# Graph layers of a relational graph network with expert layers: weight products of a finished tile spread over other couples, and a mask on numbers that are waited for

## The chip, the core and the metric

The kernel runs on one core of a Trainium2 chip. TensorE (PE) multiplies, VectorE (DVE) and ScalarE (ACT) work element by element, GpSimd (POOL) issues the gathers, and SyncE (SP) issues transfers and, in the graph layers, passes on counts. The metric is the time of one execution in microseconds. Each engine has a sequencer, which reads the program, executes register instructions and branches itself, and hands the rest to the engine.

## The reference

```python
def _rgcn_conv(x, W, Wroot, b, src, dst, etype):        # N = 6250, R = 8, 256 wide, 100000 edges
    xs = x[src]
    seg = dst * R + etype
    sums = jax.ops.segment_sum(xs, seg, num_segments=N * R)
    cnt = jax.ops.segment_sum(jnp.ones_like(xs[:, 0]), seg, num_segments=N * R)
    mean = (sums / jnp.maximum(cnt, 1.0)[:, None]).reshape(N, R, -1)
    return x @ Wroot + b + jnp.einsum('nrd,rde->ne', mean, W)

# _L0_gnn_ref
h = _rgcn_conv(x, W1, Wroot1, b1, src, dst, edge_type)
h = jax.nn.relu(h)
h = _rgcn_conv(h, W2, Wroot2, b2, src, dst, edge_type)

# the whole
x = x + _L0_gnn_ref(_layernorm(x), edge_index, edge_type_8, ...)
x = x + _L0_ffn_ref(_layernorm(x)[None], ...)[0]        # 8 experts, each row to its best 2
```

The targets `dst` are drawn with a squared uniform, so that nodes with low numbers have many edges and those with high numbers few.

## The kernel before, in words

**Stages.** The first 0.14 ms sort the edges by target and relation and normalize the rows. Then come the two graph layers, and from about 2300 us the expert layers, which the change leaves as they are (only the type of a small table of counts is another).

**A graph layer.** The sorted edges lie in 784 blocks of 128. POOL gathers each block's source rows by one indirect transfer (line 450) into a ring of 16 slots. SP waits for each landing and for each slot's last reader, and passes both on as counts (lines 355 and 362). The 6250 nodes are 49 tiles of 128. A tile is 8 windows of 16 nodes times 8 relations, so that a window has 128 sums. Two windows are a couple, and a tile has 4 couples, k = 0 to 3. For each window PE multiplies two blocks with a selection matrix of zeros and ones that DVE makes (`sel`, line 890; two matmuls a block, lines 1234 and 1235). A window that spans more than two blocks runs a loop over the further ones (`more_sums`, line 1237), with matrices that DVE makes in a loop of its own (`sel_more`, line 898). Which block comes first in a window and how many follow is read from a table into registers at each tile's start (line 1227), on PE and on DVE.

**After a couple's sums.** PE's first weight product behind them raises `sums_done`. DVE then takes the counts' inverse (layer 1), the selections of the couple after next (line 890) and those of further blocks of the next couple; ACT scales the sums to means in half precision and DVE their remainder (lines 589 and 933). One couple later PE turns the means by 8 transposes (line 1246, `turn`), and ACT copies them to `means` (line 561, counted by `means_in`).

**The weight products.** When the four couples of a tile are turned, they are multiplied by the weights: 18 parts (8 relations and the root, two halves each) of 3 matmuls (line 1254). They are strewn between the blocks of the next tile and of the one after: `couple` gives each couple a list of parts, and `spread` says how many stand at each of five places: behind the first block of the first window, behind its second, behind its further blocks, behind the first block of the second window, and behind all sums. The list is 2 parts at k = 1, 6 at k = 2 and 5 at k = 3 of the next tile, and 5 at k = 0 of the one after. Between the sums and the parts of k = 1, PE waits for `means_in`. Tiles 0 and 1 are written out, the others are a loop over pairs of tiles (`graph_tiles`). `turn`, `product` and `sums_out` (DVE's read of a finished tile's products) are the other names that matter below.

**Register instructions.** A wait for a count that depends on the table needs the number computed first: in `couple` the first block plus 2, in `more_sums` the count before plus 1, in `more_blocks` (DVE) the block plus 1, and on SP a number loaded from `free_meta`.

Of the kernel before, what the change touches and what calls it, by code (L numbers as in the profile page):

```python
def build_program(nc, x, src, dst, edge_type, gnn_w, gnn_root, gnn_bias,
# [5 lines left out]
    f32, f16, i32 = mybir.dt.float32, mybir.dt.float16, mybir.dt.int32  # L7
# [31 lines left out]
    PITCH = 2 * D + 4  # L39
    WSH, KSH = WIN.bit_length() - 1, P.bit_length() - 1  # L40
# [21 lines left out]
    PART_PAIRS = ((0, 0), (0, 1), (1, 0))  # L62
    Z_BITS, TOP, X_BITS = 8, 13, 8
# [13 lines left out]
    with ctx:  # L77
# [60 lines left out]
        lot_meta = sb("lot_meta", [1, X + 1, 4], i32)  # L138
# [176 lines left out]
        def _(sp):  # L315
# [34 lines left out]
            for layer in range(2):  # L350
# [7 lines left out]
                with sp.Fori(0, TURNS - 1) as u:  # L358
                    sp.load(regs, free_meta[0:1, ds(u * RING, RING)])
                    for s in range(RING):  # L360
                        sp.wait_ge(steps_done[layer], sp.snap(regs[s], donate=True, min_val=1, max_val=BLOCKS + 3 * WINDOWS))
                        sp.sem_inc(slots_free[layer], 1)
                        landed(u if s < AHEAD else u + 1, (s + AHEAD) % RING)
# [149 lines left out]
        def _(act):  # L513
# [45 lines left out]
            for layer in range(2):  # L559
# [19 lines left out]
                def tile_work(t, par, age):  # L579
                    for k in range(STEPS):  # L580
# [7 lines left out]
                        for h in range(2):  # L588
                            act.activation(mean16[:, slot, h, 0:D], ps_sum[slot][h][:, 0:D], ACT.Copy, scale=inv[:, ds(c * 2 + h, 1)]).then_inc(mean_high[layer], 1)  # L589
                        if age > 0 or k > 0:  # L590
                            act.wait_ge(turn_done[layer], c)
                            turned(1 - slot, par if k else 1 - par, (k - 1) % STEPS)
                        if layer == 0:
# [3 lines left out]
                            if k == 2 and age == 2:  # L597
                                relu_rows(t - 2, par)
# [91 lines left out]
        def _(v):  # L690
# [187 lines left out]
            def load_meta(w, count):  # L878
# [3 lines left out]
                lo = [v.snap(regs[2 * k], donate=True, min_val=0, max_val=BLOCKS - 1) for k in range(count)]  # L882
# [6 lines left out]
            def first_blocks(layer, lo, w, slot, h):  # L889
                return v.scalar_tensor_tensor(sel[:, slot, h], lane16[:].unsqueeze(1).to_broadcast([P, 2, P]), win_off[:, ds(w, 1)],  # L890
                                              key_tab[:, ds(lo, 2)].unsqueeze(2).to_broadcast([P, 2, P]), ALU.add, ALU.is_equal)

            def more_blocks(layer, lo, since, upto, w):
                with v.If(upto > since):
                    with v.Fori(0, upto - since) as i:
                        block = (lo + i + 2).with_bounds(min_val=0, max_val=BLOCKS - 1)
                        v.wait_ge(rows_ready[layer], block + 1)
# [3 lines left out]
            for layer in range(2):  # L901
# [11 lines left out]
                def tile_work(t, par, age):  # L913
                    regs, lo, mark = load_meta(t * WPT + 2, WPT + 2)
                    for k in range(STEPS):
# [19 lines left out]
                        if k == 1 and age == 2:  # L935
                            sums_out(t - 2, par)
                        if layer == 0:
# [4 lines left out]
                            if k == 2:  # L942
# [233 lines left out]
        def _(pe):  # L1176
# [47 lines left out]
            def load_meta(w):  # L1224
# [3 lines left out]
                lo = [pe.snap(regs[2 * k], donate=True, min_val=0, max_val=BLOCKS - 1) for k in range(WPT)]  # L1228
                return regs, lo, [pe.snap(regs[2 * k + 1], donate=True, min_val=0, max_val=BLOCKS) for k in range(WPT + 1)]

            for layer in range(2):
# [19 lines left out]
                def product(par, part):  # L1251
# [3 lines left out]
                                      start=part == 0 and n == 0, stop=part == PARTS - 1 and n == 2, skip_group_check=True)  # L1255
# [163 lines left out]
```

## Time and profile before

| | |
|---|---|
| median of 3 runs | 3062.41 us (3062.01 to 3065.25) |
| profiled execution, first to last instruction | 3064.4 us |
| PE matmul / PE weight load busy | 77% / 58% |
| DVE / ACT / POOL busy | 58% / 38% / 60% |
| layer 1 of the graph, gathers to last product | about 141 to 1199 us |
| layer 2 of the graph | about 1207 to 2290 us |

### The profile page before, as it was taken

The page shows a single profiled execution, that of the slowest core. Times are in us where ns is not written, and L with a number is a line of the kernel's source. Part 1 is how long each engine was busy: PE and PEld are TensorE (multiplying, and loading weights), DVE is VectorE, ACT ScalarE, POOL GpSimd, SP SyncE. Part 2 cuts the span into 40 slices and gives each one's busy share as a digit, 9 for nine tenths or more (in the row PEclk, how much of TensorE's full clock was granted, in tenths as well). Part 3 has the DMA queues.
Part 4 walks back from the last instruction along what each step waited for, and adds up shares of the span by engine and source line. Part 5 has one row for each costly group of instructions (what it writes and reads, how often), then busy time and mean ns, then how long its engine had stood idle before and what let it go on. Part 6 is the DMA issues. An engine that isn't in the chain of part 4 may idle for free.

```text
span 3064.4 us, 82720 instructions
## 1 busy us (share of the span) xinstructions
PE 2352.2 (77%) x19212; PEld 1776.0 (58%) x19213; DVE 1782.2 (58%) x4944; ACT 1167.6 (38%) x2306; POOL 1836.5 (60%) x1908
## 2 busy tenths in 40 slices
PE   1456777778888887456777888888987189999999
PEld 0123444555666775123445556667776178888888
DVE  7434445555566664333445555656666278877777
ACT  5001223334445553011223344455542165655554
POOL 1777777766666553777777777666536623333333
PEclk9556789999999998557899999999995599999999
DMA  7343333333333321333343444333335432322222
GB/s 244 100 130 105 108 108 108 109 101 99 97 94 93 90 88 58 106 99 115 115 119 118 123 122 125 112 113 111 106 110 192 146 123 86 100 72 72 72 72 61
DMA packets 164416, 331.14 MB, mean 108 GB/s; under 512 B 35518, under 2 KB 101786, under 8 KB 164216
## 3 DMA queue, kind: packets, MB, share of 16 engines
q0 software_dynamic: 90864, 245.38, 26.9%
q1 hardware_dynamic: 39608, 41.02, 4.5%
q10 hardware_dynamic: 33872, 43.92, 4.5%
q8 instruction: 27, 0.44, 0.1%
q14 instruction: 45, 0.37, 0.0%
HBM read 283.29 MB, written 49.07 MB: 108 GB/s over the span
## 4 chain that ended last, share of the span: by engine, by line
PE 48%; POOL 24%; issue 15%; DVE 7%; DMA 3%; DVEq 2%; ACT 1%; POOLq 0%; SPq 0%; ACTq 0%
POOL ring L450 20%; PE more_banks L1254 15%; PE sum_banks L1392 8%; PE sum_banks L1234 7%; PE sum_banks L1235 5%; PE sum_banks L1382 4%; PE more_banks L1382 4%; POOL lot_in L470 3%; PE more_banks L1246 3%; DMA ring<-table,row_tab 2%; DVE sel L890 1%; DMA out<-edge_work,lot_ids 1%; PE more_banks L1366 1%; DVEq L881 1%; DVE weights L1072 0%
## 5 line engine op out<-in xcount | busy, mean ns | idle before, releaser
L450 POOL DMA_INDIRECT ring<-table,row_tab x1568 | 1509.2, 963 | 703.8 <-issue 339.0
L1254 PE MATMUL more_banks<-weights,stage 128*128 128x256 f16 x5292 | 846.9, 283 | 7.8 <-ACT stage L561 4.5
L589 ACT ACTIVATE stage<-sum_banks,inv 128x256 f16<-128x256 f32 x784 | 327.4, 471 | 815.5 <-DVE inv L923 398.7
L1254 PEld LDWEIGHTS more_banks<-weights,stage 128*128 128x128 f16 x5292 | 502.4, 101 | 144.9 <-issue 71.6
L1234 PE MATMUL sum_banks<-ring,sel 128*128 x1568 | 449.3, 287 | 161.1 <-DVE sel L890 84.2
L898 DVE TENSOR_SCALAR sel_more<-lane,win_off,key_tab 128x128 f16 x780 | 268.8, 345 | 443.4 <-SPq L355 371.2
L1234 PE MATMUL sum_banks<-ring,sel_more 128*128 x780 | 244.3, 314 | 350.0 <-DVE sel_more L898 193.8
L890 DVE SCALAR_TENSOR_TENSOR sel<-lane,win_off,key_tab 128x256 f16<-128x256 f16 x792 | 349.4, 482 | 240.4 <-PE more_banks L1254 235.8
L1235 PE MATMUL sum_banks<-ring,sel 128*128 x1568 | 448.7, 287 | 0.0
L561 ACT ACTIVATE stage<-more_banks 128x1024 f16<-128x1024 f16 x392 | 402.7, 1027 | 15.1 <-PE more_banks L1246 14.9
L1234 PEld LDWEIGHTS sum_banks<-ring,sel_more 128*128 x780 | 78.4, 100 | 529.7 <-issue 524.9
L933 DVE SCALAR_TENSOR_TENSOR stage<-sum_banks,inv,stage 128x256 f16<-128x256 f32 x784 | 345.4, 479 | 25.8 <-issue 13.3
L1234 PEld LDWEIGHTS sum_banks<-ring,sel 128*128 128x128 f16 x1568 | 157.4, 100 | 266.5 <-issue 240.5
L489 POOL DMA_INDIRECT out<-edge_work,lot_ids x106 | 108.1, 1019 | 325.0 <-DVE edge_work L1160 308.7
L587 ACT ACTIVATE stage<-sum_banks 128x256 f16<-128x256 f32 x196 | 75.1, 383 | 591.3 <-DVE inv L923 302.1
L1235 PE MATMUL sum_banks<-ring,sel_more 128*128 x780 | 261.2, 336 | 0.0
L1246 PE MATMUL more_banks<-ident,stage 128*128 128x128 f16 x3136 | 257.3, 229 | 0.1
L665 ACT ACTIVATE stage<-sum_banks,edge_work,undo 128x256 f32<-128x256 f32 x212 | 113.0, 561 | 315.6 <-PE sum_banks L1382 294.1
L1246 PEld LDWEIGHTS more_banks<-ident,stage 128*128 128x128 f16 x3136 | 223.3, 103 | 14.0 <-DVE stage L933 1.2
L1392 PE MATMUL sum_banks<-weights,edge_work 128*128 128x256 f16 x1824 | 208.1, 275 | 7.5 <-DVE edge_work L1144 7.5
L920 DVE TENSOR_SCALAR inv<-sum_banks 128x2 f32 (+1 forms) x196 | 31.2, 159 | 290.6 <-PE more_banks L1254 276.1
L1392 PEld LDWEIGHTS sum_banks<-weights,edge_work 128*128 128x128 f16 x1824 | 179.5, 99 | 29.9 <-issue 8.4
(287 smaller groups left out, 2763.0 us busy)
## 6 DMA issues: line engine op xcount, KB each, us to landing
ring<-table,row_tab POOLq DMA_INDIRECT x1568
weights<-L_ffn_W ACTq DMA_DIRECT2D x96, 178.5 KB
stage<-L_ffn_W ACTq DMA_DIRECT2D x16, 1024.0 KB, 5.5
edge_work<-lot_in SPq DMA_DIRECT2D x54, 260.0 KB, 2.7
table<-edge_work SPq DMA_DIRECT2D x7, 896.0 KB, 4.4
table<-edge_work ACTq DMA_DIRECT2D x49, 128.0 KB
out<-acc SPq DMA_DIRECT2D x6, 1024.0 KB
acc<-x SPq DMA_DIRECT2D x6, 896.0 KB, 11.0
```

Of the source, the lines that this page charges most:

```text
L450: pool.indirect_dma_start(ring_rows[:, b % RING, 0:2 * D], None, tables[layer], bass.IndirectOffsetOnAxis(row_tab[:, b:b + 1], 0)).then_in ...
L561: act.activation(means[:, par, :, :, 2 * k * WIN:(2 * k + 2) * WIN].rearrange("p q r (v n) -> p v (q r) n", v=2), ps_turn[slot].rearrange( ...
L589: act.activation(mean16[:, slot, h, 0:D], ps_sum[slot][h][:, 0:D], ACT.Copy, scale=inv[:, ds(c * 2 + h, 1)]).then_inc(mean_high[layer], 1)
L890: return v.scalar_tensor_tensor(sel[:, slot, h], lane16[:].unsqueeze(1).to_broadcast([P, 2, P]), win_off[:, ds(w, 1)], key_tab[:, ds(lo, 2 ...
L898: v.tensor_scalar(flat(sel_more[:, ds(block & (RING - 1), 1), :]), lane16[:], win_off[:, ds(w, 1)], key_tab[:, ds(block, 1)], ALU.add, ALU ...
L933: v.scalar_tensor_tensor(mean16[:, slot, h, D:2 * D], ps_sum[slot][h][:, 0:D], inv[:, ds(c * 2 + h, 1)], mean16[:, slot, h, 0:D], ALU.mult ...
L1234: pe.matmul(to[:, 0:D + 1], hot, flat(slot[:, :, D:2 * D + 1]), start=first, stop=last, skip_group_check=True)
L1235: return pe.matmul(to[:, 0:D], hot, flat(slot[:, :, 0:D]), start=False, stop=last, skip_group_check=True)
L1246: out = [pe.transpose(ps_turn[slot][:, (4 * h + q) * P:(4 * h + q + 1) * P], mean16[:, slot, h, q * P:(q + 1) * P], ident16[:]) for h in r ...
L1254: return [pe.matmul(ps_out[par], rows[:, xp * KD + k, :], w16[:, wp, k, r * D:(r + 1) * D], start=part == 0 and n == 0, stop=part == PARTS ...
L1382: ins = pe.matmul(hid_bank[c % 4], up_sb[slot][:, wp, k, c * P:(c + 1) * P], lotT[:, zp, k, :], start=k == 0 and (wp, zp) == PART_PAIRS[0] ...
L1392: ins = pe.matmul(bank[2 + h][:, 0:D], hidT[:, hp, c, h * P:(h + 1) * P], down_sb[slot][:, wp, c, :], start=c == 0 and (hp, wp) == PART_PA ...
```

## The change

It has four parts. (1) The parts of a tile are given out as 4 at k = 2 and 5 at k = 3 of the next tile, and 5 at k = 0 and 4 at k = 1 of the one after, with the root's two parts first (`PART_ORDER`). (2) The wait for `means_in` stands at the start of k = 2, ahead of its sums. (3) DVE's `sums_out` moves from k = 1 to k = 2 and its addition of the second bias from k = 2 to k = 1; ACT's `relu_rows` moves from behind the turned copy at k = 2 to ahead of it at k = 3. (4) Every number that an engine waits for is put through `& MASK` (2047), and the bounds on the table's block numbers move to where they are used as addresses. `lot_meta` becomes a table of 16-bit integers. The end of a layer has 9 parts of the last tile but one instead of 5, and 2 parts of the last tile, ahead of the last wait.

```diff
+    MASK = (1 << (BLOCKS + 3 * WINDOWS).bit_length()) - 1
...
+    PART_ORDER = [R * KD + k for k in range(KD)] + list(range(R * KD))
+    SHARES = (5, 4, 4, 5)
+    SPREAD = {4: (1, 1, 0, 1, 1), 5: (1, 1, 1, 1, 1)}
+    CUTS = (0, SHARES[2], SHARES[2] + SHARES[3], SHARES[2] + SHARES[3] + SHARES[0], PARTS)
...
# SP
-                        sp.wait_ge(steps_done[layer], sp.snap(regs[s], donate=True, min_val=1, max_val=BLOCKS + 3 * WINDOWS))
+                        sp.wait_ge(steps_done[layer], sp.snap(regs[s], donate=True) & MASK)
...
# ACT, tile_work
+                        if layer == 0 and k == 3 and age == 2:
+                            relu_rows(t - 2, par)
                         if age > 0 or k > 0:
                             act.wait_ge(turn_done[layer], c)
                             turned(1 - slot, par if k else 1 - par, (k - 1) % STEPS)
...
-                            if k == 2 and age == 2:
-                                relu_rows(t - 2, par)
...
# DVE, more_blocks
                     with v.If(upto > since):
+                        held = v.snap(lo & MASK)
                         with v.Fori(0, upto - since) as i:
...
-                        v.wait_ge(rows_ready[layer], block + 1)
+                        v.wait_ge(rows_ready[layer], held + i + 3)
...
# DVE, tile_work
-                        if k == 1 and age == 2:
+                        if k == 2 and age == 2:
                             sums_out(t - 2, par)
...
-                            if k == 2:
+                            if k == 1:
                                 here = flat(acc[:, ds(t, 1), :])
                                 v.tensor_tensor(here, here, bias_bc[:, 1, :], ALU.add).then_inc(x_biased, 1)
...
# PE, more_sums
                     with pe.If(upto > since):
+                        done = pe.snap(since & MASK)
                         with pe.Fori(0, upto - since) as i:
-                            pe.wait_ge(more_ready[layer], since + i + 1)
+                            pe.wait_ge(more_ready[layer], done + i + 1)
...
# PE, couple
-                    if k == 0:
-                        parts = [(par, n) for n in range(PARTS - 5, PARTS)] if age == 2 else []
-                    else:
-                        parts = [(1 - par, n) for n in (range(0, 2), range(2, 8), range(8, 13))[k - 1]] if age > 0 else []
-                    spread = ((1, 1, 1, 1, 1), (0, 0, 0, 0, 2), (1, 1, 1, 1, 2), (1, 1, 1, 1, 1))[k]
+                    due = (k + 2) % STEPS
+                    of, enough = (par, age == 2) if k < 2 else (1 - par, age > 0)
+                    parts = [(of, n) for n in PART_ORDER[CUTS[due]:CUTS[due + 1]]] if enough else []
+                    spread = SPREAD[SHARES[k]]
...
+                    if k == 2 and age > 0:
+                        if age == 1:
+                            pe.wait_ge(w_split, layer + 1)
+                        pe.wait_ge(means_in[layer], t * STEPS)
...
-                        pe.wait_ge(rows_ready[layer], lo[j] + 2)
+                        pe.wait_ge(rows_ready[layer], (lo[j] & MASK) + 2)
...
-                    if k == 1 and age > 0:
-                        if age == 1:
-                            pe.wait_ge(w_split, layer + 1)
-                        pe.wait_ge(means_in[layer], t * STEPS)
...
# PE, the end of a layer
-                for n in range(PARTS - 5, PARTS):
+                for n in PART_ORDER[CUTS[2]:CUTS[3]]:
+                    product(1, n)
+                turn(COUPLES - 1, 1)
+                for n in PART_ORDER[CUTS[3]:]:
                     ins = product(1, n)[-1]
                 ins.then_inc(out_done[layer], 1)
-                turn(COUPLES - 1, 1)
+                for n in PART_ORDER[:KD]:
+                    product(0, n)
                 pe.wait_ge(means_in[layer], COUPLES)
                 if layer == 0:
                     weights_spread(1)
-                for n in range(PARTS):
+                for n in PART_ORDER[KD:]:
                     ins = product(0, n)[-1]
```

```order
L1278 REGISTER_ALU
L1280 REGISTER_ALU [waits rows_ready0]
L1234 REGISTER_ALU [waits sel_ready0]
L1234 ISA
L1234 MATMUL sum_banks<-ring,sel 128x257
L1235 ISA
L1235 MATMUL sum_banks<-ring,sel 128x256
L1234 REGISTER_ALU x2
L1234 ISA
L1234 MATMUL sum_banks<-ring,sel 128x257
L1235 ISA
L1235 MATMUL sum_banks<-ring,sel 128x256
```

The same place now.

```order
L1289 REGISTER_ALU x2
L1291 REGISTER_ALU [waits rows_ready0]
L1241 REGISTER_ALU [waits sel_ready0]
L1241 ISA
L1241 MATMUL sum_banks<-ring,sel 128x257
L1242 ISA
L1242 MATMUL sum_banks<-ring,sel 128x256
L1262 MATMUL more_banks<-weights,stage 128x256 x3
L1241 REGISTER_ALU x2
L1241 ISA
L1241 MATMUL sum_banks<-ring,sel 128x257
L1242 ISA
```

There is one register instruction more ahead of the wait for `rows_ready`, and a weight part of 3 matmuls stands behind the first block, where nothing stood. A second such instruction stands ahead of the second window's wait; over a tile's body PE has the same 138 matmuls and 16 more REGISTER_ALU, one in each of its 8 windows and one in each of the 8 further-block branches.

**PE, the end of couple k = 1 in layer 1's loop, before** (`means_in0` counts layer 1's turned copies, `mean_low0` its remainders).

```order
L1239 ISA
L1239 COMPARE_AND_BRANCH
L1238 UNCONDITIONAL_BRANCH
L1254 MATMUL more_banks<-weights,stage 128x256 [waits means_in0]
L1254 MATMUL more_banks<-weights,stage 128x256 x5
L1245 ISA
L1246 MATMUL more_banks<-ident,stage 128x128 [waits mean_low0]
L1246 MATMUL more_banks<-ident,stage 128x128 x7
```

What stands between the turn of k = 1 and the first block of k = 2 now, where the wait has gone.

```order
L1254 MATMUL more_banks<-ident,stage 128x128 x7
L1281 ISA
L1281 MATMUL sum_banks<-ident,edge_work 128x128
L1281 ISA
L1281 MATMUL sum_banks<-ident,edge_work 128x128
L1289 REGISTER_ALU [waits means_in0]
L1289 REGISTER_ALU
L1291 REGISTER_ALU [waits rows_ready0]
L1241 REGISTER_ALU [waits sel_ready0]
L1241 ISA
```

The wait stands on a register instruction ahead of k = 2, behind the turn and the root's transposes, no longer on the products behind the sums of k = 1; those are 3 matmuls now and were 6.

**DVE, a branch for further blocks in layer 2, before and now.**

```order
L894 COMPARE_AND_BRANCH
L895 UNCONDITIONAL_BRANCH
L895 ISA
L898 REGISTER_ALU [waits rows_ready1]
L898 REGISTER_ALU
L898 ISA
L898 TENSOR_SCALAR sel_more<-lane,win_off,key_tab 128x128
L895 ISA
```

```order
L900 COMPARE_AND_BRANCH
L902 UNCONDITIONAL_BRANCH
L904 REGISTER_ALU
L904 ISA
L905 ISA [waits rows_ready1]
L905 REGISTER_ALU
L905 ISA
L905 TENSOR_SCALAR sel_more<-lane,win_off,key_tab 128x128
L902 ISA
```

One register instruction more stands in the branch ahead of the loop, and in the loop the number that is waited for comes from an ISA instead of a REGISTER_ALU.

## Rows read from the trace of the kernel before

**Rows 1.** The page, part 4: shares of the span on the chain that ended last.

```profile
PE 48%; POOL 24%; issue 15%; DVE 7%; DMA 3%; DVEq 2%; ACT 1%; POOLq 0%; SPq 0%; ACTq 0%
```

**Rows 2.** By stretch, gathers (L450) alone: from:to us, POOL busy (count), PEclk, DMA share, GB/s.

```profile
300.00:586.00 286.00, 216.86 (x228) 0.87 0.37 108
586.00:1190.00 604.00, 368.84 (x384) 0.99 0.31 92
1480.00:1896.00 416.00, 315.47 (x329) 0.94 0.41 120
1896.00:2290.00 394.00, 225.89 (x237) 1.00 0.36 107
```

**Rows 3.** The same view, transposes (L1246) alone: PE busy (count) PEld busy (count), PEclk.

```profile
586.00:1190.00 604.00, 91.50 (x1191) 79.52 (x1187) 0.99 0.31 92
1480.00:1896.00 416.00, 50.85 (x608) 44.41 (x608) 0.94 0.41 120
1896.00:2290.00 394.00, 65.26 (x856) 56.79 (x856) 1.00 0.36 107
1050.00:1190.00 140.00, 24.40 (x320) 21.23 (x320) 1.00 0.26 75
```

**Rows 4.** Timeline, PE, one late tile of layer 2: start, us, line, count [idle <-releaser].

```profile
2252.40 0.61 PE L1246 MATMUL more_banks<-ident,stage 128*128 128x128 f16 x8
...
2255.86 0.61 PE L1246 MATMUL more_banks<-ident,stage 128*128 128x128 f16 x8
...
2256.68 0.28 PE L1234 MATMUL sum_banks<-ring,sel 128*128 x1
...
2257.44 0.28 PE L1234 MATMUL sum_banks<-ring,sel 128*128 x1 [0.36 <-issue]
2257.56 0.28 PE L1235 MATMUL sum_banks<-ring,sel 128*128 x1
2257.89 0.28 PE L1234 MATMUL sum_banks<-ring,sel 128*128 x1
...
2258.96 0.61 PE L1246 MATMUL more_banks<-ident,stage 128*128 128x128 f16 x8
...
2262.36 0.61 PE L1246 MATMUL more_banks<-ident,stage 128*128 128x128 f16 x8
...
2265.32 0.61 PE L1246 MATMUL more_banks<-ident,stage 128*128 128x128 f16 x8
```

**Rows 5.** PE sequencer's instructions, whole span, by line: count, ns min/median/max.

```profile
L1278 PEldq ALU_OP  x784: 36/36/36, 96.8 to 2275.4; - x196
...
L1239 PEldq MOVE  x390: 29/29/29, 98.1 to 2276.5; - x195
...
L1227 PEldq TENSOR_LOAD <-meta x98: 1356/1361/1377, 95.3 to 2264.5; - x98
```

**Rows 6.** Entries into the further-block loop, by stretch (586:1190, 1480:1896, 1896:2290).

```profile
L1239 PEldq MOVE  x99: 29/29/29, 588.6 to 1186.9; - x99
...
L1239 PEldq MOVE  x126: 29/29/29, 1484.7 to 1895.8; - x126
...
L1239 PEldq MOVE  x39: 29/29/29, 1900.6 to 2276.5; - x39
```

**Rows 7.** Waits, 586 to 1190 us: engine line <- releaser: us in total, times, longest.

```profile
DVE inv L920 <- PE more_banks L1254: 183.7, 149, 3.5
PE sum_banks L1234 <- DVE sel_more L898: 14.4, 15, 1.5
PEld more_banks L1254 <- ACT stage L561: 6.2, 14, 1.1
```

**Rows 8.** Waits, 1480 to 1896 us.

```profile
DVE sel_more L898 <- SPq L355: 80.9, 70, 3.2
PE sum_banks L1234 <- DVE sel_more L898: 23.0, 35, 1.3
```

**Rows 9.** Timeline, the end of layer 1.

```profile
1193.13 6.07 PE L1254 MATMUL more_banks<-weights,stage 128*128 128x256 f16 x54
```

More of the change, by code:

```diff
@@ L5, in build_program @@
     from concourse import mybir
-    f32, f16, i32 = mybir.dt.float32, mybir.dt.float16, mybir.dt.int32
+    f32, f16, i32, u16 = mybir.dt.float32, mybir.dt.float16, mybir.dt.int32, mybir.dt.uint16
     ALU, ACT, AX = mybir.AluOpType, mybir.ActivationFunctionType, mybir.AxisListType
@@ L62, in build_program @@
     PART_PAIRS = ((0, 0), (0, 1), (1, 0))
+    PART_ORDER = [R * KD + k for k in range(KD)] + list(range(R * KD))
+    SHARES = (5, 4, 4, 5)
+    SPREAD = {4: (1, 1, 0, 1, 1), 5: (1, 1, 1, 1, 1)}
+    CUTS = (0, SHARES[2], SHARES[2] + SHARES[3], SHARES[2] + SHARES[3] + SHARES[0], PARTS)
+    assert CUTS[3] + SHARES[1] == PARTS
     Z_BITS, TOP, X_BITS = 8, 13, 8
@@ L137, in build_program @@
         extremes = sb("extremes", [P, 2, SCANS])
-        lot_meta = sb("lot_meta", [1, X + 1, 4], i32)
+        lot_meta = sb("lot_meta", [1, X + 1, 4], u16)
         raw_i = ring[0:NAT, 0:4 * ROW].bitcast(i32).rearrange("g (a e) -> g a e", a=4)
@@ L881, in load_meta @@
                 v.load(regs, meta_row[0:1, ds(2 * w, 2 * count)])
-                lo = [v.snap(regs[2 * k], donate=True, min_val=0, max_val=BLOCKS - 1) for k in range(count)]
+                lo = [v.snap(regs[2 * k], donate=True) for k in range(count)]
                 return regs, lo, [v.snap(regs[2 * k + 1], donate=True, min_val=0, max_val=BLOCKS) for k in range(count)]
@@ L890, in first_blocks @@
                 return v.scalar_tensor_tensor(sel[:, slot, h], lane16[:].unsqueeze(1).to_broadcast([P, 2, P]), win_off[:, ds(w, 1)],
-                                              key_tab[:, ds(lo, 2)].unsqueeze(2).to_broadcast([P, 2, P]), ALU.add, ALU.is_equal)
+                                              key_tab[:, ds(lo.with_bounds(min_val=0, max_val=BLOCKS - 1), 2)].unsqueeze(2).to_broadcast([P, 2, P]), ALU.add, ALU.is_equal)
             def more_blocks(layer, lo, since, upto, w):
                 with v.If(upto > since):
+                    held = v.snap(lo & MASK)
                     with v.Fori(0, upto - since) as i:
                         block = (lo + i + 2).with_bounds(min_val=0, max_val=BLOCKS - 1)
-                        v.wait_ge(rows_ready[layer], block + 1)
+                        v.wait_ge(rows_ready[layer], held + i + 3)
                         v.tensor_scalar(flat(sel_more[:, ds(block & (RING - 1), 1), :]), lane16[:], win_off[:, ds(w, 1)], key_tab[:, ds(block, 1)],
@@ L1227, in load_meta @@
                 pe.load(regs, meta_row[0:1, ds(2 * w, 2 * WPT + 4)])
-                lo = [pe.snap(regs[2 * k], donate=True, min_val=0, max_val=BLOCKS - 1) for k in range(WPT)]
+                lo = [pe.snap(regs[2 * k], donate=True) for k in range(WPT)]
                 return regs, lo, [pe.snap(regs[2 * k + 1], donate=True, min_val=0, max_val=BLOCKS) for k in range(WPT + 1)]
@@ L1254, in product @@
                     return [pe.matmul(ps_out[par], rows[:, xp * KD + k, :], w16[:, wp, k, r * D:(r + 1) * D],
-                                      start=part == 0 and n == 0, stop=part == PARTS - 1 and n == 2, skip_group_check=True)
+                                      start=part == PART_ORDER[0] and n == 0, stop=part == PART_ORDER[-1] and n == 2, skip_group_check=True)
                             for n, (xp, wp) in enumerate(PART_PAIRS)]
```

## The prediction

> **What bounds the kernel now.** I read the chain of waits first. PE holds 48%, POOL 24% and "issue" 15% [rows 1]: no engine alone, and a good part is time in which an engine waits for nothing but its own sequencer. So I cut the two graph layers into stretches and read two things in each, the pace of the gathers and that of the tiles (a tile has 32 transposes).
>
> Where POOL never waits, a gather takes 286 / 228 = 1.25 us (300 to 586 us) [rows 2]. From 1480 to 1896 it is 416 / 329 = 1.26, so layer 2 is bound by POOL, or nearly, to about 1896 us. Layer 1 leaves that pace at about 586: 604 / 384 = 1.57. Layer 2 has 394 / 237 = 1.66 behind 1896. In these last two stretches something on PE's side sets the time: 1191 / 32 = 37.2 tiles in 604 us, and 856 / 32 = 26.8 tiles in 394 us [rows 3].
>
> It is not the array. A late tile of layer 2 without further blocks takes 2265.32 - 2252.40 = 12.92 us [rows 4]. Its array work is 54 product matmuls and 32 block matmuls at 0.11 us each (54 in a row take 6.07 with the last one's 0.27) [rows 9] and 36 transposes at half of that: 9.4 + 2.0 = 11.4 us. Nor is it DVE, which waits 183.7 us of 604 for PE [rows 7]. It is PE's sequencer. In couple k = 1 nothing stands between the blocks, and there its pace is bare: second block to the next window's first 2256.68 to 2257.44, 0.76 us; first to second block 2257.44 to 2257.89, 0.45 [rows 4]. That is 1.21 us a window and 9.7 us for eight, to which come the table load of 1.36 us [rows 5] and some 18 register instructions for turns, roots and waits, 1.9 us: 13.0 us, the tile's time. The sequencer runs nearly without a pause, and the array's work lies beside it. (Line 1239's MOVE opens the further-block loop; each entry adds instructions, which is why earlier tiles take longer.)
>
> **The price of a masked number.** Nothing in the trace is a mask, but the same kind of instruction is there. From the second matmul of a block (2257.56) to the next block (2257.89) are 0.33 us with two REGISTER_ALU and one ISA, from 2257.44 to 2257.56 are 0.12 with one ISA [rows 4]: (0.33 - 0.12) / 2 = 0.105 us each. The recorded execution is 36 ns [rows 5]. Those are the two ends for one instruction, and I take 0.105, since it is a distance between starts of what is issued.
>
> The Trainium skill bears on that choice (Perfetto Trace Analysis, Sequencer-only Instruction): the profile shows only the execution of such an instruction, and fetching and pushing come on top before the next can be fetched. By it the 36 ns are not the price; the spacing in the rows agrees.
>
> **The change part by part.**
>
> *Masks on PE.* One in each window (784, as line 1278) and one at each entry into the further-block loop (390 in all, of which 99, 126 and 39 in the three stretches) [rows 5, 6].
> - Layer 1 from 586: 37.2 x 8 + 99 = 397 instructions x 0.105 = 41.7 us, all on the sequencer that sets the time.
> - Layer 2 from 1896: 26.8 x 8 + 39 = 253 x 0.105 = 26.6 us.
> - Layer 2, 1480 to 1896: 19 x 8 + 126 = 278 x 0.105 = 29.2 us. Here POOL and the sequencer run level: DVE waits 80.9 us for landed blocks, PE only 23.0 for DVE's selections [rows 8]. Both ends, 0 and 29.2, are possible; I take half, 14.6.
> - The other 1174 - 928 = 246 lie in the early tiles, under POOL's pace: 0 to 25.8, I take 2, for there the slack is widest.
>
> Sum: +84.9 us.
>
> *Masks elsewhere.* DVE has one more instruction at each of 390 entries, at most 390 x 0.105 = 41 us, covered by its wait for PE [rows 7] save where PE waits for a selection: 14.4 us in 15 cases of layer 1 [rows 7], so 1 us. Some of PE's own masks ahead of such a wait are swallowed by it: 264 + 126 entries at most, I count 6 us back. SP's mask stands once per block, between events 1.25 us or more apart: 0; should SP be late, POOL's next gather waits, 0.1 us a block, 784 x 2 x 0.1 = 157 us at the outside, which nothing suggests.
>
> *The parts spread out.* No matmul is added. k = 1 had no part between its blocks and 2 behind, and the array idled there (0.36 us before 2257.44) [rows 4]; k = 2 had 6 and took 3.40 us (2258.96 to 2262.36), which is array work; k = 1 takes 3.10 with the same register instructions, so 0.3 us of k = 2 is the array's. With 4 parts its array work is 3.40 - 2 x 0.33 = 2.74, and the sequencer's 3.1 + 0.2 takes its place. So filling k = 1's holes gives little: they are hidden under a sequencer that must issue the blocks anyway. What comes back is the sequencer's wait for an array that is behind at the end of k = 3: 0.2 us a tile, 37 x 0.2 = 7 in layer 1 and 5 in layer 2. With the array less behind, `sums_done` also comes sooner and the waits for `sel_more` shrink: half of 14.4 [rows 7], 7, and 3 in layer 2.
>
> *The wait for the turned copies.* At k = 1 it costs 6.2 us in layer 1 [rows 7]; at the start of k = 2, some 0.8 us of sequencer time later, ACT is done: -6. Late tiles of layer 1 take 140 / 10 = 14.0 us [rows 3] against the 12.92 of layer 2's, so there is room for this. What is queued behind the moved wait is the whole of k = 2, so a late ACT would now hold blocks too; 0 to +4, I take 0.
>
> *DVE's and ACT's moved operations* are the same operations in neighbouring couples of engines that wait for PE: 0, between -3 and +3. *The end of a layer*: 6 parts now stand in the wait ahead of the last 54 matmuls (6.07 us) [rows 9], and 48 remain; 4 of the 6 are added there, so it is 0.3 us a layer: -0.6. *The expert layers*: 0.
>
> Total: 84.9 + 1 - 6 - 12 - 10 - 6 - 0.6 = +51. The profiled execution has 3064.4 us and would have 3115; the median, 2 us below it, gives **3113 us**, 1.7% more.
>
> **The rivals.**
>
> *A, faster: the sequencer runs ahead and hides the masks.* PE's queue holds work while the sequencer goes on, so with parts in every couple the array might never run dry. Then the masks cost nothing and the gain is what I count back plus the array's bare waits for issue at tile starts, 0.3 us x 64 tiles = 19: -12 -10 -6 -19 = -47, 3015 us. It decides if the sequencer has more than 0.84 us of slack in a tile; 13.0 us of instructions in a tile of 12.92 speak against it.
>
> The Trainium skill gives this rival its footing (TensorE: Matmul & The Clock Gate, Architectural detail): TensorE's queue holds 64 instructions. Such a queue hides register work only where the array has a backlog, and at the array's 11.4 us a tile against the sequencer's 13 no backlog lasts.
>
> *B, no change: the give-back is as large as the masks.* If the lopsided parts cost layer 1 1 us a tile and layer 2 0.8, 37 + 21, and POOL hides all before 1896, then 41.7 + 26.6 - 58 - 6 = +4: 3066 us. For it: layer 1's late tiles, at 14.0 us, stand above 12.92, though further blocks explain part. The point from which it decides: more than 1 us a tile given back.
>
> *C, slower still: everything is exposed.* All 1174 masks at 0.105 are 123 us, less 34 back: +89, 3151 us. For it: POOL's 1.26 us in layer 2 has next to no slack. Against: before 586 POOL's pace is not PE's to set.
>
> **How the numbers follow.** Mine 0.69, A 0.09, B 0.10, C 0.12. Mine alone would run from 3090 to 3135. The range of 8 in 10 takes in C and most of the way to B: 3078 to 3152. A measurement tells about 0.2%, 6 us, from no change. Faster: A, 0.09. Same: most of B, 0.08. Slower: the rest, 0.83.
>
> **What would show it.** In the profile after, gathers stay at 1.25 us before 586, and the stretch of POOL's pace in layer 2 ends earlier than 1896. The tile of 12.92 us becomes about 13.5; between the two blocks of a window it is still 0.45, but from a window's second block to the next window's first 0.76 becomes 0.86 where nothing is queued. Late tiles of layer 1 take 14.0 to 14.5. Products no longer wait for ACT's line 561. I am wrong if the late tiles keep 12.92 us or fall: then the sequencer had slack, or masks cost only their 36 ns (+29 in place of +85, and near no change in sum). The expert layers must take as long as before; if not, the table's 16 bits matter.

## The result and the profile after

The changed kernel takes 3222.66 us (median of 4 runs, 3216.72 to 3231.86), the kernel before 3062.31 beside it: a ratio of 1.0522 with a 95% interval of 1.0504 to 1.0541. It is slower, as I said, but by 160 us where I had said 51, and outside the range of 3078 to 3152. The span of the profiled execution is 3221.2 us.

Three views carry the reading. First the chain that ended last (the page, part 4):

```profile
PE 56%; issue 20%; DVE 9%; POOL 8%; DVEq 3%; DMA 2%; ACT 1%; POOLq 0%; SPq 0%; ACTq 0%
```

Against [rows 1] POOL fell from 24% to 8%, PE and "issue" took its place. The stages that POOL had paced are paced by something else, and that is the first thing I had excluded. The gathers alone say where (300 to 586 us, columns as in [rows 2]):

```profile
300.00:586.00 286.00, 191.72 (x202) 0.81 0.34 96
```

202 gathers where there were 228, 1.42 us each instead of 1.25. TensorE's granted clock is lower there too, 0.81 against the 0.87 of [rows 2]; what of the loss is the clock's, no run separates. In the same stretch POOL now waits for a free slot of the ring:

```profile
POOL ring L456 <- SPq L368: 60.4, 91, 3.0
```

Before, the same wait came to this much in the same 286 us:

```profile
POOL ring L450 <- SPq L362: 8.8, 29, 0.3
```

Slots come free when TensorE has finished a block, so it is TensorE's side that is late. The turns (eight transposes) date the loss. In the timeline of before, the turn of tile 12's second couple in layer 1 (its 50th turn) and the last turns of layers 1 and 2 start at:

```profile
603.15 0.61 PE L1246 MATMUL more_banks<-ident,stage 128*128 128x128 f16 x8
...
1191.02 0.62 PE L1246 MATMUL more_banks<-ident,stage 128*128 128x128 f16 x8
...
2280.39 0.61 PE L1246 MATMUL more_banks<-ident,stage 128*128 128x128 f16 x8
```

The same three of after:

```profile
654.75 0.61 PE L1254 MATMUL more_banks<-ident,stage 128*128 128x128 f16 x8
...
1272.57 0.62 PE L1254 MATMUL more_banks<-ident,stage 128*128 128x128 f16 x8
...
2432.22 0.61 PE L1254 MATMUL more_banks<-ident,stage 128*128 128x128 f16 x8
```

52 us are lost by tile 12 alone, where my sum had 2 for the early tiles of both layers. By the end of layer 1 it is 81.5, by the end of layer 2 151.8, and of the spans' 156.8 the last 5 come behind the graph layers.

What the sequencer of TensorE executes explains it (the source view, by line; L1247 is the further-block loop, L1239 of before; L1248 the wait in it; L1289 the window's wait, L1278 of before):

```profile
L1247 PEldq MOVE  x1170: 29/37/38, 99.2 to 2428.6; - x195
...
L1248 PEldq ALU_OP  x780: 36/36/36, 99.4 to 2428.8; - x195
L1248 PEldq FUSED_REGOPS  x780: 41/41/41, 99.5 to 2428.9; - x195
...
L1289 PEldq ALU_OP  x1568: 36/36/36, 97.9 to 2427.4; - x196
```

The windows' 784 masks are there as expected: 1568 for the 784 of [rows 5]. But the loop has 1170 MOVEs for 390, and 780 ALU_OPs that before has not. `done = pe.snap(since & MASK)` stands ahead of the loop in the source, and the compiled program computes it again in each round: a copy and a mask, 780 times, not once in 390 entries. TensorE issues 2344 instructions more, not 1174, and the second half of them where my sum had put the least, in the loop of further blocks: of its 780 rounds 474 lie ahead of 586 us or between 1190 and 1480. VectorE's loop has the same two (L902, L895 before):

```profile
L902 DVEq MOVE  x1170: 36/36/48, 97.5 to 2427.1; - x195
```

The order of instructions above shows this for VectorE: `L904 REGISTER_ALU` is the mask, line 904 is the wait inside the loop, and it stands behind the loop's head. I had read it as standing ahead of the loop.

A late tile of layer 2 without further blocks is the part that I had worked out closely. In the timeline, turn to turn, with the starts of two windows between:

```profile
2402.75 0.61 PE L1254 MATMUL more_banks<-ident,stage 128*128 128x128 f16 x8
...
2407.02 0.61 PE L1254 MATMUL more_banks<-ident,stage 128*128 128x128 f16 x8
...
2410.11 0.61 PE L1254 MATMUL more_banks<-ident,stage 128*128 128x128 f16 x8
2410.71 0.28 PE L1241 MATMUL sum_banks<-ring,sel 128*128 x1
...
2411.27 0.27 PE L1241 MATMUL sum_banks<-ring,sel 128*128 x1
...
2412.01 0.28 PE L1241 MATMUL sum_banks<-ring,sel 128*128 x1
...
2412.58 0.27 PE L1241 MATMUL sum_banks<-ring,sel 128*128 x1
...
2413.21 0.61 PE L1254 MATMUL more_banks<-ident,stage 128*128 128x128 f16 x8
...
2416.17 0.61 PE L1254 MATMUL more_banks<-ident,stage 128*128 128x128 f16 x8
```

It takes 2416.17 - 2402.75 = 13.42 us (predicted: about 13.5), against the 12.92 of [rows 4]. From a window's second block to the next window's second are 1.31 us, where it took 1.21. Not every couple is longer: by the turns the first one, which holds the table load, goes from 3.46 to 4.27 us, the third from 3.40 to 3.10, and the two others stay within 0.01.

The 5 us behind the graph layers I put down to the expert table; no run has it alone. Its loads of four values were 331 to 339 ns (L1371 before) and are, now that it holds 16-bit values:

```profile
L1382 PEldq TENSOR_LOAD <-lot_meta x8: 982/984/1012, 2600.3 to 3201.4; - x8
```

### The profile page after: what moved, and what is told of

It is laid out like the page before. It is cut to its first block, busy times and chain, and to the rows that moved or that the text cites. A ratio compares the mean times of both kernels' runs of the same rounds, so it can differ in the third digit from the quotient of the medians.

```text
span 3221.2 us, 88160 instructions
## 1 busy us (share of the span) xinstructions
PE 2389.7 (74%) x19212; PEld 1766.1 (55%) x19213; DVE 1781.3 (55%) x4944; ACT 1166.9 (36%) x2306; POOL 1838.1 (57%) x1908
## 4 chain that ended last, share of the span: by engine, by line
PE 56%; issue 20%; DVE 9%; POOL 8%; DVEq 3%; DMA 2%; ACT 1%; POOLq 0%; SPq 0%; ACTq 0%
PE more_banks L1262 17%; PE sum_banks L1241 12%; PE sum_banks L1242 8%; PE sum_banks L1403 7%; POOL ring L456 5%; PE sum_banks L1393 4%; PE more_banks L1393 4%; PE more_banks L1254 4%; POOL lot_in L476 3%; DVE sel L896 2%; DVE sel_more L905 2%; DVEq L905 1%; PE sum_banks L1281 1%; DMA out<-edge_work,lot_ids 1%; PE more_banks L1377 1%
## 5 line engine op out<-in xcount | busy, mean ns | idle before, releaser
L1262 PE MATMUL more_banks<-weights,stage 128*128 128x256 f16 x5292 | 895.9, 285 | 1.2
L1241 PE MATMUL sum_banks<-ring,sel 128*128 x1568 | 456.5, 291 | 200.3 <-DVE sel L896 112.5
L1241 PE MATMUL sum_banks<-ring,sel_more 128*128 x780 | 249.4, 320 | 436.4 <-issue 282.2
L896 DVE SCALAR_TENSOR_TENSOR sel<-lane,win_off,key_tab 128x256 f16<-128x256 f16 x792 | 349.0, 482 | 348.3 <-PE more_banks L1262 330.1
L905 DVE TENSOR_SCALAR sel_more<-lane,win_off,key_tab 128x128 f16 x780 | 261.8, 336 | 437.8 <-SPq L361 283.6
L1242 PE MATMUL sum_banks<-ring,sel 128*128 x1568 | 456.8, 291 | 0.1
L1242 PE MATMUL sum_banks<-ring,sel_more 128*128 x780 | 267.8, 343 | 0.0
```

The source lines that it names most:

```text
L905: v.tensor_scalar(flat(sel_more[:, ds(block & (RING - 1), 1), :]), lane16[:], win_off[:, ds(w, 1)], key_tab[:, ds(block, 1)], ALU.add, ALU ...
L1241: pe.matmul(to[:, 0:D + 1], hot, flat(slot[:, :, D:2 * D + 1]), start=first, stop=last, skip_group_check=True)
L1242: return pe.matmul(to[:, 0:D], hot, flat(slot[:, :, 0:D]), start=False, stop=last, skip_group_check=True)
L1262: return [pe.matmul(ps_out[par], rows[:, xp * KD + k, :], w16[:, wp, k, r * D:(r + 1) * D], start=part == PART_ORDER[0] and n == 0, stop=p ...
```

## The experiments

All ratios are to the kernel before, run on the same chip beside them; a per mille is 3 us.

**Which part of the change.** Four kernels between before and after. tables_only is before with its three tables in 16 bits and no mask; the other two without masks build on it.

```
tables_only : meta, free_meta, lot_meta: i32 -> u16
parts_only  : after, meta and free_meta in u16, waits on the bare numbers
masks_only  : before + all masks + lot_meta in u16 (old shares)
pe_loop     : tables_only + done = pe.snap(since & MASK); wait_ge(.., done + i + 1)
```

> The kernel before, with its three tables of counts (block numbers and further blocks of each window, readers of a slot, rows of an expert) kept as 16-bit instead of 32-bit integers, no mask and the old shares of products. Theory (PE's sequencer and the register instructions it executes set the tiles' time): the same register instructions, so 3062 us, within 5. Rival (the table's loads are on the path and their width matters): 98 loads of 1.36 us on PE, up to 30 us away from 3062.

> The changed kernel without any mask (16-bit tables instead): only the new shares, the moved wait and the moved DVE and ACT operations. Theory (masks cost all, parts gain a little): 3062 - 27 = 3035 us, between 3020 and 3055. Rival (the parts hold back sums_done and the selections behind it, and are most of the 160 us): 3100 us or more.

> The kernel before with all masks on PE, DVE and SP as the change has them, old shares, old waits. Theory: the measured 3223 plus what the parts give back, 3223 + 27 = 3250 us; the two alone add up to the change within 10 us. Rival (the parts are at fault): 3150 us or less.

> The kernel before on 16-bit tables, with the mask on the number that PE waits for in its loop over further blocks alone. The trace of the changed kernel has two more sequencer instructions in each of the 780 rounds of that loop, 0.193 us a round. Theory: 780 x 0.193 = 150 us at most, less what POOL's pace of 1.25 us a gather still hides: +90 to +120, about 3165 us, the larger half of the change. Rival (DVE's masks ahead of its selections are the larger half): +40 or less, 3100 us.

Measured: tables_only 1.1343 (1.1324 to 1.1362), parts_only 1.1277 (1.1258 to 1.1295), masks_only 1.0553 (1.0535 to 1.057), pe_loop 1.1618 (1.1598 to 1.1637).

The first missed by 411 us: the form of the table was to cost nothing. Its trace shows where most of it comes from, in the load of the 20 values of a tile that took 1.36 us [rows 5]:

```profile
L1227 PEldq TENSOR_LOAD <-meta x98: 4717/4730/5209, 95.2 to 2666.5; - x98
```

98 x 3.37 = 330 us on TensorE's sequencer, and 411 in the time. The loads of VectorE (line 881, 100 of them, median 1.36 to 4.48 us) and of SyncE (line 359, 96 of them, 0.97 to 3.26) grew too, so the 411 are not TensorE's alone; that a load of 16-bit values is dear stands. This makes tables_only a poor base in size, and parts_only and pe_loop, expected at 3035 and 3165 us, miss with it; what can be read are the differences to it. The shares, the moved wait and the moved operations together save 20 us (parts_only), and the one masked expression in TensorE's loop costs 84 us (pe_loop), a little under the 90 to 120 expected. masks_only puts the blame: the masks with the expert table lose 170 us without the new shares, and the shares give back only 10 of them (0.0031, with the two intervals' 0.0025 either way), where I had expected 27.

**Taking instructions out one kind at a time.** Four kernels built on after, first on a chip where everything was slower.

```
dose        : wait_ge(rows_ready, ((lo[j] & (2*MASK+1)) & MASK) + 2)    # PE, +784 ALU_OP
lean_window : table holds block + 2: wait_ge(rows_ready, lo[j] & MASK)   # PE, -784 ALU_OP
              (ring slots and meta moved by 2 to match; VectorE looks up its keys at lo - 2)
lean_loop   : wait_ge(more_ready, (since + i + 1) & MASK), no `done`     # PE, -780 MOVE
lean        : both, and VectorE's wait on (lo + i + 1) & MASK
```

> The changed kernel with a second mask in each of the 784 window waits of PE and nothing else. Theory (each register instruction on PE's sequencer costs the 0.0965 us at which such instructions start behind one another, and the sequencer is the bound from the first tiles on): +784 x 0.0965 = +76 us at most, 3223 + 60 to 76, about 3290 us. Rival (early tiles go at POOL's 1.25 us a gather, so only the 64 late tiles pay): +49 us, 3272. Rival (the 36 ns that the profile records are the price): +28 us, 3251.

> The changed kernel with the table holding the block number plus 2, so that a window's wait needs the mask alone and no addition (the ring of gathered blocks is turned by two slots to match): 784 PE instructions fewer, the masks of the loops stay. Theory: the mirror image of the doubled mask, 3223 - 60 to 76, about 3155 us. Rival (the early tiles are POOL's): -45 us, 3178.

> The changed kernel with PE's mask in the further-block loop put on the sum (the count before plus the round plus 1, masked) and not on the count before; by the trace of the changed kernel the latter costs a MOVE and an ALU_OP in each of 780 rounds, the former should cost the ALU_OP alone. A round then takes 1.17 us, again under POOL's 1.25. Theory: -780 x 0.096 = -75 us at most, and as POOL's pace comes back into force less: -40 to -60, about 3172 us. Rival (DVE's loop, which has the same two instructions more, sets the pace of the rounds): -10 or less, 3213.

> Both of these, and the same for DVE's loop. Theory: PE has 780 ALU_OP more than the kernel before and nothing else, so 3062 + 5 for the slower 16-bit table of the experts - 15 for the new shares + 0 to 75: about 3095 us, between 3070 and 3125. Rival (what is lost lies with the shares or with SP's masks): above 3150.

On that chip the kernel before itself took 3515.2 us, 450 more than elsewhere, and these 1.0421 (1.0394 to 1.0448), 1.0216 (1.0187 to 1.0245), 1.0207 (1.0178 to 1.0237) and 1.0166 (1.0128 to 1.0205). Its traces show single register instructions held up, here those of the loop in dose, whose longest in after is 38 ns:

```profile
L1247 PEldq MOVE  x1170: 3/35/728, 98.6 to 2828.9; - x195
```

Why, I can't tell from here. dose is the slowest and lean the fastest of the four, as expected; the two between can't be told apart, the sizes are not usable, and I ran dose, lean_window and lean again on another chip, with a fifth kernel:

```
lean_more : lean, running count + 1 in the table: wait_ge(more_ready, (since + i) & MASK)
```

> The kernel after with a second mask in each window: 784 ALU_OPs more. If the sequencer is the bound in all of both graph layers, +60 to +76 us over 1.0522: ratio 1.072 to 1.077. If only late tiles count (64 of 98), +49: 1.068. If a queue hides it, 1.052.

> The kernel after without the 784 adds behind the window masks; the loop's copy and mask stay (2 instructions in each of 780 rounds). Count theory: 3222 less 784 x 0.0965 = 76, less what POOL's pace gives no room for in the early tiles: 3147 to 3175, ratio 1.028 to 1.037. Rival: my prediction's price with the loop entries counted once would leave it at +30 to +40, 1.01.

> As lean_more, but the table holds the count itself, so each round of TensorE's further-block loop has one ALU_OP more (780). At 0.0965 us each, hidden under POOL's pace at worst before 586 us: +25 to +75 over lean_more. On the chip where all kernels ran 15% longer lean stood at 1.0166; the count theory expects 1.010 to 1.02 here, the rival (only the first few hundred instructions matter) the same as lean_more.

> The kernel after, with the same bounds on the waited numbers but no instruction more on TensorE's sequencer than the kernel before: the table holds block + 2 and the running count + 1, so that a window waits on one masked number (one ALU_OP, as the sum was) and a further block on (since + i) & MASK (one fused pair, as the sum of three was); no MOVE in a round. VectorE's loop keeps one instruction more a round. If the sequencer's instruction count is all of the loss, the 156 us of it go and what is left is the new parts (-11 to -20), the 16-bit expert table (+5) and VectorE (0 to +10): ratio 0.993 to 1.002. If a mask is dear of itself, or the new parts cost something that the masks hid, 1.01 or more.

Measured: dose_again 1.0736 (1.0718 to 1.0754), window_again 1.0304 (1.0287 to 1.0321), lean_again 1.0198 (1.0181 to 1.0215), lean_more 1.0206 (1.0189 to 1.0223).

784 ALU_OPs more cost 0.0214, 66 us; 784 fewer give back 0.0218, 67 us: 0.084 us each, in both directions (window_again also has 184 subtractions more on VectorE). The early tiles pay too: at layer 1's 50th turn the traces stand 4.3 us behind after and 8.1 ahead of it. No queue hides them. lean_again has the ratio that I gave it, but not the distance of 25 us or more to lean_more, and lean_more missed by 0.02. lean_more was not what I had called it: its trace has one ALU_OP for each round beyond before, exactly as lean_again has, since the pair was not fused:

```profile
L1246 PEldq ALU_OP  x780: 36/36/36, 98.6 to 2332.2; - x195
```

So the two have the same instructions on TensorE, and some 60 us over before were left. The last turn of layer 1 starts at 1190.31 us in lean_more, 0.7 ahead of before's, so what was left at the end was lost in layer 2. There VectorE stands still for nothing that the profile shows (waits of VectorE in lean_more, 1440 to 2347 us):

```profile
DVE sel L896 <- issue: 102.8, 28, 5.3
```

in the timeline:

```profile
2240.79 0.88 DVE L896 SCALAR_TENSOR_TENSOR sel<-lane,win_off,key_tab 128x256 f16<-128x256 f16 x2 [4.75 <-issue]
```

and the queue that carries instructions has moved more than after's 46 packets:

```profile
q14 instruction: 155, 1.27, 0.1%
```

The 110 packets more fall in layer 2, 5 in each of 22 passes of its loop over pairs of tiles. lean, lean_again and lean_more had put a subtraction into VectorE's code for a tile, to undo the + 2 of the table. That made a new theory: the code of a tile no longer stays where VectorE keeps it, and is fetched anew.

**Settling the rest.**

```
lean_keys       : lean_more, key table moved by two columns: no subtraction on VectorE
lean_pe         : lean_keys with VectorE's loop as in after (held = v.snap(lo & MASK))
lean_old_shares : lean_keys with before's shares and before's places of the ACT wait and of the
                  moved DVE and ACT operations
wait_back       : after, wait_ge(means_in, ..) back from couple 2 to the end of couple 1
```

> As lean_more, with the table of keys shifted by two columns too, so that VectorE's code loses the subtraction that lean_more put ahead of each window's first selections (4 in the code of a tile). lean_more needed layer 1 as long as before, and lost 55 us in layer 2, where VectorE stood still up to 5 us at a time and the instruction queue moved 155 packets where after has 46. If that is code that VectorE fetches again in each tile, its packets go back to about 46 and the time to 3062 to 3075, ratio 0.998 to 1.003. If layer 2 lost to something else, it stays at 1.02.

> TensorE as in lean_keys, VectorE's loop as in the kernel after (the copy and the mask in each of 780 rounds: 2 instructions a round more than in lean_keys, less one). If the loss is TensorE's alone: within 0.3% of lean_keys. If VectorE's rounds pace the early tiles too, 10 to 30 us above it.

> lean_keys with the parts of before: none between the blocks of couple 1 and six in couple 2, and the wait for the turned copies in couple 1. The difference to lean_keys is what the new shares are worth: by my prediction 18 + 10 + 0.6 = 28 us less the array's share, so 15 to 29 us above lean_keys; by the comparisons so far (20 with the 16-bit tables, 11 with the masks) 10 to 20.

> The kernel after with the wait for the turned copies back at the end of couple 1, where before had it; shares unchanged. I priced its move at -6 us: expectation +3 to +6, ratio 1.053 to 1.054. Rival: the move is what relieves the late tiles of layer 1 altogether, +15 or more.

Measured: lean_keys 1.0016 (1.0006 to 1.0025), lean_pe 1.0046 (1.0028 to 1.0064), lean_old_shares 1.0087 (1.0069 to 1.0105), wait_back 1.0522 (1.0493 to 1.0551).

lean_keys confirms that the fetching and the loss go together: four instructions fewer in VectorE's code for a tile of layer 2 (184 executed, 8 in each pass of the loop), 0.019 (58 us) less time, "sel L896 <- issue" gone from VectorE's waits in layer 2, and the instruction queue is back at

```profile
q14 instruction: 45, 0.37, 0.0%
```

lean_pe differs from window_again on TensorE by its loop alone, and the row of the loop shows what went:

```profile
L1246 PEldq MOVE  x390: 29/29/34, 98.6 to 2305.1; - x195
```

780 MOVEs fewer, 1.0304 to 1.0046, 79 us: 0.10 us each, if the 184 subtractions that VectorE loses at the same step cost nothing. The same two instructions a round turned into one on VectorE are worth 9 us (lean_pe to lean_keys), 6 either way. Shares, moved wait and moved operations together are worth 22 us (lean_old_shares to lean_keys), 6 either way. The move of the wait for ACT by itself is worth nothing that can be measured.

Last, the two masks not yet priced, each doubled in lean_keys:

```
sp_dose  : sp.wait_ge(steps_done, (reg & (2*MASK+1)) & MASK)
dve_dose : v.wait_ge(rows_ready, ((lo + i + 1) & (2*MASK+1)) & MASK)
```

> lean_keys with a second mask on SyncE's waited number, one more ALU_OP for each gather that waits for a free slot (1504). My prediction costed SyncE's mask at 0. If it is on the path between a finished block and the next gather, +0.1 us at some of the gathers that wait for their slot: +3 to +20 us, mostly before tile 12 of each layer; if it is not, ratio as lean_keys, 1.0016 within 0.1%.

> lean_keys with a second mask in each round of VectorE's loop (780 ALU_OPs). From lean_pe (+11 us for one instruction more a round) I expect +8 to +15 us, ratio 1.004 to 1.0065, and 45 to 47 packets in the instruction queue. If the eight instructions that it adds to the code of a tile bring it over the size at which VectorE fetches again, 155 packets and +45 or more.

Measured: sp_dose 1.0025 (1.0016 to 1.0034), dve_dose 1.0049 (1.0036 to 1.0062). The two ran on another chip than lean_keys, so each is set against it by the ratios to before. A second mask on SyncE costs 3 us, with intervals that allow 0 and 7; one in each of VectorE's rounds costs 10 us, 5 either way.

dve_dose also answers the theory of the code's size, and against it. It has 8 instructions more than lean_keys in the code of a tile, where lean_more had 4 more; window_again has lean_more's subtractions and one instruction more than lean_more in each further-block branch besides. Both have longer code for a tile of layer 2 than lean_more, no such stalls, and each has

```profile
q14 instruction: 46, 0.38, 0.0%
```

So the number of instructions does not decide whether the code is fetched again. Where it lies might; no run tests that, and the cause stays open.

lean_old_shares is 27 us over before. If VectorE's first mask costs what the second did, 10, the expert table 3 to 5 and SyncE's mask up to 3, some 10 are left for TensorE's own 780 masks, about 0.01 us each against the 0.10 of the next 780. That is a remainder of numbers with intervals of 5 us and more, and not shown. The shortest round, by the starts of the loop's instructions, takes 1.07 us in before, 1.17 in lean_keys and 1.27 in after, and POOL's gather takes 1.25. It is tempting to say that an instruction is free up to that pace and dear beyond it. The traces speak against so sharp a line. A round is not a gather: 1568 gathers serve 2348 blocks on TensorE, since a block on the border of two windows is multiplied for both. And in lean_old_shares, whose shortest round is 1.16 us, the early tiles are already slower (gathers alone, 300 to 586 us):

```profile
300.00:586.00 286.00, 212.56 (x222) 0.86 0.37 106
```

That is 1.29 us a gather, and layer 1's 50th turn is 13.0 us later than in before. What the first 780 masks of TensorE's loop cost by themselves stays open.

## Why the prediction was wrong in size

- **What bounds the kernel**: right for the late tiles. The sequencer sets the time behind 586 and behind 1896 us, and the doses, equal in both directions, show it better than my sum of a tile did. It was wrong that POOL's pace keeps TensorE's instructions out of the time elsewhere.
- **The price of a mask, 0.105 us**: right. Starts are 0.096 to 0.097 us apart in the trace after; the time moves by 0.084 (windows) and 0.10 (MOVEs).
- **How many there are: a step that failed.** "One at each entry into the further-block loop (390 in all)". It is two in each of 780 rounds. The expression had to be looked for in the compiled loop; I read it by the source. With 784 + 1560 in place of 1174 the spacing in the trace gives 2344 x 0.0965 = 226 us gross.
- **"The other 246 lie in the early tiles, under POOL's pace; I take 2": the step that failed by most.** The count alone would not have taken the time out of my range: with the instructions of the table below and my own cover, 2 us early and half of the stretch from 1480, the masks come to 110 us instead of 84.9, and the time to 3138. What failed is the cover. The early tiles were to hide nearly all of it and did not; I had tested no point at which the cover ends.

| stretch of before, us | instructions in my sum | instructions more, by trace | masks in my sum, us | loss measured, us |
|---|---|---|---|---|
| layer 1 to 586 | 246, with 1190 to 1480 | 678 | 2, with 1190 to 1480 | 50.9 |
| 586 to 1190 | 397 | 494 | 41.7 | 30.6 |
| 1190 to 1480 | in the 246 | 396 | in the 2 | 8.8 |
| 1480 to 1896 | 278 | 485 | 14.6 | 38.5 |
| 1896 to 2290 | 253 | 291 | 26.6 | 23.0 |

The instructions are the windows and twice the loop's rounds in each stretch; the loss is the difference of the same turn's start in the two timelines at the stretch's ends, with the masks of VectorE and SyncE and what the new shares give back already in it. The early tiles of layer 1 cost most, and 16.5 of their 50.9 us stand at the layer's first turn; those of layer 2 cost 8.8. Why the two layers differ there, no run shows.

- **Stretch 1480 to 1896**: half of the two ends, 14.6 us. It lost 38.5, with 485 instructions in place of 278: at 0.105 that is 51 us gross, so most of them came out in the time.
- **VectorE: +1 us** was short for the same reason. It had 1560 instructions more and not 390. Taking one of the two out of each round gave 9 us, doubling the one that was left cost 10, and neither was done in the kernel after itself.
- **SyncE: 0.** The doubled mask cost 3 us, 0 and 7 not excluded: near right.
- **The shares: -12 -10 -0.6**, and the wait's -6, 28.6 us. The runs take all of it out together: 22 (lean_keys), 20 (tables_only); but only 10 between masks_only and after. The size was nearly right where few masks stand in the way. I take it that with a sequencer far behind the array never is, so nothing is there to give back; no run shows that.
- **The wait for the turned copies: -6.** Not seen: putting it back changed nothing (1.0522 both), but with an interval of 0.3% or 9 us, so 6 us are neither shown nor excluded.
- **Expert layers: 0.** Measured +5, and +3 in the traces of masks_only, lean_keys and lean_old_shares; I put it down to the 16 bits of the table. I had named that as the sign, not as a cost.
- **Rival C** (all exposed, 3151 us) was nearest, and had the right mechanism for the early tiles with half of the instructions. Rival A (a queue hides them) is refuted by the doses; B needed 58 us given back, and 10 to 22 were. That the kernel became slower was forecast from the right mechanism; the size was not.

Signs: the late tile (13.42) came as written, and a window's 1.31 us are the 0.45 + 0.86 of the forecast. The split did not show: it is 0.57 and 0.74, since a part now stands behind each first block. In the tile the sum came right and the couples did not (k = 2 was to take 3.3 us and took 3.10). "gathers stay at 1.25 us before 586" did not, and is the one that would have told me first.

No version here beats before. The nearest, lean_keys, keeps the bounds and the new shares, and is 1.6 per mille slower; what it gains by the shares, 22 us, the remaining masks and the expert table take.

## What to carry to other kernels

Where an engine's sequencer sets the pace, count its instructions in the compiled program, by line and by execution: a value computed ahead of a loop in the source may be computed again in each round. Before calling such an instruction hidden, work out how much the hiding engine leaves free in that stage, per unit of the same work, and how much the change adds: here 678 instructions, some 65 us, went into a stage of 445 us, and 51 came out. Part of the cost can show before the cover is used up. A bound on a number that already passes through an addition costs TensorE no instruction more if the table is made to hold the sum.

## What the runs showed of the hardware

- An ALU_OP recorded with 36 ns takes TensorE's sequencer 0.096 to 0.097 us from start to start, a MOVE recorded with 29 to 37 ns 0.088 to 0.095. In the kernel's time they cost 0.084 us (784 more or fewer ALU_OPs) and 0.10 us (780 MOVEs).
- A register load of 16-bit values is about three times as long as one of 32-bit values: 4 values 0.984 against 0.333 us, 20 values 4.73 against 1.36. By differences that is 0.234 us a value against 0.064. No run here shows why.
- With four instructions more in VectorE's code for a tile, it fetched code again in each pass of layer 2's loop: 155 instruction packets for 45, 28 stalls of 3.7 us (102.8 us in all), 58 us of the kernel's time. Two kernels with still more instructions there (dve_dose, window_again) did not, at 46 packets, so the count alone is not the cause.
- The same program took 3515 us on one chip and 3062 to 3068 on the others, with register instructions of up to 0.73 us; what disturbed them stays open.
